# Spreading query and key halves over partitions by DMA, with the attention steps laid out anew

## The reference

```python
x = x + 0.5 * ffn(layernorm(x))      # silu(x W1^T) * (x W3^T), Walsh-Hadamard over 2048, times W2^T
x = x + attention(layernorm(x))
x = x + 0.5 * ffn(layernorm(x))

# attention, per head h and chunk; the weights are quantised to -1, 0, 1 times a scale
scores = einsum('bhtd,bhsd,hts->bhts', qi, ki, mask)      # mask: exp(-s_h (t - s)) below the diagonal
intra  = einsum('bhts,bhsd->bhtd', scores, vi)
cross  = einsum('bhtd,ht,bhde->bhte', qi, lam_t, S)
S      = lam_T * S + einsum('bhtd,ht,bhte->bhde', ki, lam_rev, vi)
out    = rmsnorm(rmsnorm(scale * (intra + cross))) @ proj^T
```

## Time and profile before

| | |
|---|---|
| profiled execution | 2532.32 us |
| its span, first to last instruction | 2530.6 us |
| median of three runs | 2535.62 us |
| TensorE matmul busy | 2385.3 us, 94% |
| VectorE busy | 1351.3 us, 53% |
| ScalarE busy | 873.9 us, 35% |
| mean granted TensorE clock | 0.987 |

### The profile page before, as it was taken

How to read it: one execution, slowest core, us unless ns; L and a number is a source line. 1 busy time by engine, 2 the same in 40 slices (tenths; PEclk the granted TensorE clock), 3 DMA queues, 4 the chain that set the end, 5 groups by cost and what they waited for, 6 DMA issues and landing times.

```text
span 2530.6 us, 32351 instructions
## 1 busy us (share of the span) xinstructions
PE 2385.3 (94%) x13040; PEld 1144.2 (45%) x13040; DVE 1351.3 (53%) x2599; ACT 873.9 (35%) x1461; POOL 161.5 (6%) x111
## 2 busy tenths in 40 slices
PE   5786999999999999999999999999999999989999
PEld 2243454445444454444544445444544445445444
DVE  6766565346644466335653466444664347557612
ACT  5545442234322352224522243223432245235211
POOL 4710000000000000000000000000000000000000
PEclk9898999999999999999999999999999999999999
DMA  7732002010012001100020100210002000100100
GB/s 218 178 109 57 1 1 50 17 34 1 17 34 34 17 1 32 36 17 17 1 51 17 34 1 5 46 26 25 1 17 49 19 17 1 34 17 1 34 17 17
DMA packets 184533, 82.58 MB, mean 33 GB/s; under 512 B 166080, under 2 KB 166080, under 8 KB 184384
## 3 DMA queue, kind: packets, MB, share of 16 engines
q1 hardware_dynamic: 184384, 80.51, 13.5%
HBM read 31.20 MB, written 8.39 MB: 16 GB/s over the span
## 4 chain that ended last, share of the span: by engine, by line
PE 77%; DVE 14%; issue 4%; DMA 2%; ACT 1%; POOL 1%; SPq 0%; POOLq 0%; DVEq 0%; ACTq 0%
PE l_bank L1262 23%; PE g_bank L1262 22%; PE d_bank L1277 22%; PE a_bank L1318 3%; DVE work L834 3%; PE a_bank L1304 2%; PE a_bank L1385 2%; DVE work L969 1%; PE a_bank L1372 1%; PE a_bank L1336 1%; DMA work<-cent 1%; DVE cent L1094 1%; PE a_bank L1366 1%; DVE stat L1031 1%; DVE stat L1028 1%
## 5 line engine op out<-in xcount | busy, mean ns | idle before, releaser
L1277 PE MATMUL d_bank<-w2t,work 128*128 128x512 f16 x2976 | 685.7, 381 | 10.9 <-DVE work L976 10.9
L969 DVE SCALAR_TENSOR_TENSOR work<-l_bank,l_scale,work 128x512 f32<-128x512 f32 x256 | 191.6, 749 | 649.0 <-PE l_bank L1262 647.6
L1277 PEld LDWEIGHTS d_bank<-w2t,work 128*128 128x128 f16 x2976 | 289.9, 98 | 352.7 <-DVE work L976 11.9
L1262 PE MATMUL l_bank<-xt,w3t 128*128 128x512 f16 x1728 | 404.5, 384 | 31.4 <-DVE work L969 31.4
L1262 PE MATMUL g_bank<-xt,w1t 128*128 128x512 f16 x1728 | 400.6, 382 | 19.6 <-ACT work L719 13.4
L719 ACT ACTIVATE work<-g_bank,g_scale 128x512 f32<-128x512 f32 x256 | 175.3, 685 | 506.9 <-PE g_bank L1262 504.1
L732 ACT CAST work<-work 128x512 f16<-128x512 f32 x248 | 153.2, 618 | 470.8 <-DVE work L969 469.6
L1262 PE MATMUL g_bank<-work,w1t 128*128 128x512 f16 x1344 | 308.4, 379 | 0.0
L1262 PE MATMUL l_bank<-work,w3t 128*128 128x512 f16 x1344 | 308.4, 379 | 0.0
L1262 PEld LDWEIGHTS l_bank<-xt,w3t 128*128 128x128 f16 x1728 | 168.1, 99 | 231.5 <-issue 45.1
L1262 PEld LDWEIGHTS g_bank<-xt,w1t 128*128 128x128 f16 x1728 | 167.4, 98 | 215.9 <-ACT work L719 13.0
(11 more groups left out here) (196 smaller groups left out, 1721.3 us busy)
## 6 DMA issues: line engine op xcount, KB each, us to landing
w2t<-in_L_ffn_W_dram SPq DMA_DIRECT2D x32, 256.0 KB, 3.3
xin<-in_L_attn_x_dram SPq DMA_DIRECT2D x8, 1024.0 KB, 5.2
out_dram<-work SPq DMA_DIRECT2D x7, 1024.0 KB, 4.3
work<-in_L_ffn_W_dram SPq DMA_DIRECT2D x8, 512.0 KB, 4.6
w2t<-in_L_attn_qkv_w_dram SPq DMA_DIRECT2D x6, 512.0 KB, 4.7
work<-in_L_attn_qkv_w_dram SPq DMA_DIRECT2D x3, 1024.0 KB, 7.9
mask<-in_L_attn_x_dram SPq DMA_DIRECT2D x1, 1024.0 KB, 5.7
w2t<-in_L_attn_proj_w_dram SPq DMA_DIRECT2D x2, 512.0 KB, 3.9
```

Of the source, the lines that this page charges most:

```text
L969: nc.vector.scalar_tensor_tensor(out=hfull, in0=l_bank[:], scalar=l_scale[:, j:j + 1], in1=gate, op0=ALU.mult, op1=ALU.mult).then_inc(hful ...
L1262: ins = nc.tensor.matmul(dst[:], wt[:, wp, k, P * j:P * (j + 1)], src[:, xp, k, :], start=(k == 0 and wp == xp), stop=(k == KT - 1 and wp ...
L1277: ins = nc.tensor.matmul(d_bank[t][:], parts[:, hp, P * t:P * (t + 1)], w2t[:, wp, j, :], start=(j == 0 and hp == wp), stop=(j == HT - 1 a ...
```

## The change

q_parts, k_parts and kT become buffers of their own. The two halves of q and of k are each stored to a DRAM buffer by SyncE (256 KB), and loaded from there three times each into 32 partitions of qs or ks (128 KB). The loads of a group wait until the last score of the group before has been computed. For groups 1 to 3, q moves to the slot of the group before's score 1, k to the slot of its score 2, and the low half of k to that of score 3. In group 0 the four value steps come before kturn and the first score. The attention starts its first score one slot later. The list NORM goes; its steps stand in the first three slots of the first attention block, as in the last one.

```diff
@@ -94,8 +94,10 @@
         sc = at["sc"].bitcast(F16).rearrange("p (b a h t) -> p b a h t", b=2, a=2, h=HG)
-        q_parts = sc[:, 0].rearrange("p a h t -> p a (h t)")
-        k_parts = sc[:, 1].rearrange("p a h t -> p a (h t)")
+        q_parts = sb("q_parts", [P, 2, T], F16)
+        k_parts = sb("k_parts", [P, 2, T], F16)
+        kT = sb("kT", [P, T])
+        parts_dram = nc.dram_tensor("parts_dram", [2, 2, P, 2, T], F16, kind="Internal").ap()
         def values(buffer):
...
@@ -233,18 +236,18 @@
         def attention_slots(at):
             slots = {}
-            start = at + 4
+            start = at + 5
             for g in range(GROUPS):
                 b = start + (3 + TT) * g
-                lead = b - 4 if g == 0 else b - 3
-                add(slots, lead, [("q", g)])
-                add(slots, lead + 1, [("qlow", g), ("k", g)])
-                add(slots, lead + 2, [("klow", g), ("kturn", g)])
+                lead = 6 if g else 5
+                add(slots, b - lead, [("q", g)])
+                add(slots, b - lead + 1, [("qlow", g), ("k", g)])
+                add(slots, b - lead + 2, [("klow", g)])
                 if g == 0:
-                    add(slots, b - 1, [("v", 0), ("v", 1)])
+                    add(slots, b - 3, [("v", 0), ("v", 1)])
+                    add(slots, b - 2, [("v", 2), ("v", 3)])
+                add(slots, b - 1, [("kturn", g)])
                 add(slots, b, [("score", (g, 0))])
-                if g == 0:
-                    add(slots, b, [("v", 2), ("v", 3)])
                 add(slots, b + 1, [("kv", g), ("score", (g, 1)), ("state", g)])
                 for c in range(TT):
                     add(slots, b + 2 + c, [("pv", (g, c))] + ([("score", (g, c + 2))] if c < TT - 2 else []))
@@ -274,7 +277,7 @@
                 add(slots, at + 5, tr1)
             return slots
-        def last_attention_slots():
+        def late_attention_slots():
             slots = attention_slots(4)
             pre, tr0, tr1 = norm_steps("qkv")
             return {**slots, 0: pre, 1: tr0, 2: tr1}
@@ -338,12 +341,11 @@
             return steps + [("resid", ("ffn1", t)) for t in range(TT)]
         FIRST = first_steps()
-        WITH_FIRST_ATTENTION = feed_forward("ffn1", attention_slots(4))
+        WITH_FIRST_ATTENTION = feed_forward("ffn1", late_attention_slots())
         WITH_ATTENTION = feed_forward("ffn1", attention_slots(0))
         SECOND = feed_forward("ffn2", second_slots())
-        SECOND_WITH_ATTENTION = feed_forward("ffn2", last_attention_slots())
+        SECOND_WITH_ATTENTION = feed_forward("ffn2", late_attention_slots())
         LAST = feed_forward("ffn2", {})
-        NORM = [step for steps in norm_steps("qkv") for step in steps]
         def bank_use(step, arg):
@@ -414,7 +416,7 @@
             return isinstance(v, int) and v <= 0
-        PLAN = [(FIRST, dict()), (NORM, dict(ffn=1))]
+        PLAN = [(FIRST, dict())]
         for i in range(1, B):
             PLAN.append((WITH_FIRST_ATTENTION if i == 1 else WITH_ATTENTION, dict(ffn=2 * i - 1, attn=i - 1, block=i, loaded=i)))
@@ -524,6 +526,33 @@
                         sp.wait_ge(res_done, TT * (place.ffn + 1))
                         sp.dma_start(out_tiles[bass.ds(place.block * TT, TT)].rearrange("t p d -> p t d"), x2).then_inc(y_stored, 16)
+                    elif step == "qlow":
+                        ag = place.attn * GROUPS + arg
+                        sp.wait_ge(q_lo, ag + 1)
+                        if ag >= 2:
+
+                            sp.wait_ge(q_moved, 16 * BLOCKS * (ag - 1))
+                        sp.dma_start(parts_dram[ag % 2, 0], q_parts[:]).then_inc(q_stored, 16)
+                    elif step == "klow":
+                        g = arg
+                        ag = place.attn * GROUPS + g
+                        sp.wait_ge(k_lo, ag + 1)
+                        if ag >= 2:
+
+                            sp.wait_ge(k_moved, 16 * BLOCKS * (ag - 1))
+                        sp.dma_start(parts_dram[ag % 2, 1], k_parts[:]).then_inc(k_stored, 16)
+                        if g:
+
+                            b, fill = place.filled("score", (g - 1, TT - 1))
+                            sp.wait_ge(a_ready[b], fill)
+                        sp.wait_ge(q_stored, 16 * (ag + 1))
+                        for i, part in enumerate((0, 1, 0)):
+                            sp.dma_start(qs[HD * i:HD * (i + 1)],
+                                         parts_dram[ag % 2, 0, :, part].rearrange("(h p) t -> p h t", h=HG)).then_inc(q_moved, 16)
+                        sp.wait_ge(k_stored, 16 * (ag + 1))
+                        for i, part in enumerate((0, 0, 1)):
+                            sp.dma_start(ks[HD * i:HD * (i + 1)],
+                                         parts_dram[ag % 2, 1, :, part].rearrange("(h p) t -> p h t", h=HG)).then_inc(k_moved, 16)
                     elif step == "split":
                         which, t = arg
                         m = place.norm[which]
...
@@ -763,22 +786,22 @@
                         nc.scalar.mul(qT[:], a_bank[b][:], QKV_SCALE / X_SCALE).then_inc(a_free[b], 1)
                         act.wait_ge(a_free[b], place.copied(step, arg, b) + 1)
+                        if ag:
+                            act.wait_ge(q_stored, 16 * ag)
                         nc.scalar.copy(q_parts[:, 0, :], qT[:]).then_inc(q_hi, 1)
-                        act.wait_ge(q_hi, ag + 1)
-                        move_high(q_parts, qs).then_inc(q_moved, 1)
                     elif step == "k":
                         b, fill = place.filled(step, arg)
                         ag = place.attn * GROUPS + arg
                         act.wait_ge(a_ready[b], fill)
                         if not known_zero(ag):
-                            act.wait_ge(sc_lo, TT * ag)
-                        nc.scalar.mul(flow, a_bank[b][:], QKV_SCALE / X_SCALE).then_inc(a_free[b], 1)
+                            act.wait_ge(kd_lo, ag)
+                        nc.scalar.mul(kT[:], a_bank[b][:], QKV_SCALE / X_SCALE).then_inc(a_free[b], 1)
                         act.wait_ge(a_free[b], place.copied(step, arg, b) + 1)
-                        nc.scalar.copy(k_parts[:, 0, :], flow).then_inc(k_hi, 1)
-                        act.wait_ge(k_hi, ag + 1)
-                        move_high(k_parts, ks).then_inc(k_moved, 1)
+                        if ag:
+                            act.wait_ge(k_stored, 16 * ag)
+                        nc.scalar.copy(k_parts[:, 0, :], kT[:]).then_inc(k_hi, 1)
                     elif step == "v":
                         t = arg
                         b, fill = place.filled(step, arg)
...
@@ -1057,10 +1074,10 @@
                         m = place.norm[which]
                         src = norm_source(place, which)[:, t, :]
                         dve.wait_ge(ln_rstd, m + 1)
-                        if place.steps is NORM:
+                        if place.steps is WITH_FIRST_ATTENTION and (which, t) == ("qkv", 0):
                             for b in range(2):
-                                dve.wait_ge(a_free[b], place.copied(step, arg, b))
+                                dve.wait_ge(a_free[b], place.copies[b])
                         if t and not (place.steps is FIRST and which == "ffn1"):
@@ -1109,17 +1126,11 @@
                         ag = a * GROUPS + arg
                         dve.wait_ge(q_hi, ag + 1)
                         nc.vector.tensor_tensor(q_parts[:, 1, :], qT[:], q_parts[:, 0, :], ALU.subtract).then_inc(q_lo, 1)
-                        move(q_parts, qs, 2, 0)
-                        dve.wait_ge(q_lo, ag + 1)
-                        move(q_parts, qs, 1, 1).then_inc(q_moved, 1)
                     elif step == "klow":
                         ag = a * GROUPS + arg
                         dve.wait_ge(k_hi, ag + 1)
-                        nc.vector.tensor_tensor(k_parts[:, 1, :], flow, k_parts[:, 0, :], ALU.subtract).then_inc(k_lo, 1)
-                        move(k_parts, ks, 1, 0)
-                        dve.wait_ge(k_lo, ag + 1)
-                        move(k_parts, ks, 2, 1).then_inc(k_moved, 1)
+                        nc.vector.tensor_tensor(k_parts[:, 1, :], kT[:], k_parts[:, 0, :], ALU.subtract).then_inc(k_lo, 1)
                     elif step == "v":
                         t = arg
...
                         n_sc = TT * (a * GROUPS + g) + c
                         b, fill = place.filled(step, arg)
                         dve.wait_ge(a_ready[b], fill)
-                        if c:
+                        if n_sc:
                             dve.wait_ge(sc_lo, n_sc)
-                        else:
-                            dve.wait_ge(kd_lo, a * GROUPS + (g + 1))
                         masked = flow.rearrange("p (h t) -> p h t", h=HG)
                         nc.vector.scalar_tensor_tensor(out=masked, in0=a_bank[b][:].rearrange("p (h t) -> p h t", h=HG),
```

(14 more changed lines are left out.)

9 lines of the change are left out of this document (5 added, 4 removed).

## The result

The changed kernel takes 2547.60 us (median of five, 2546.31 to 2551.20) against 2535.62: a ratio of 1.005, 95% interval 1.0036 to 1.0065. That is 12.0 us slower, where +2.4 was forecast; it lies in the stated range of 2527 to 2557, but beyond the likeliest case's own 2531 to 2545.

What follows compares the result with a forecast made beforehand. The prediction took TensorE's in-order queue as the bound, so only its waits count: 53.8 - 46.6 - 3.2 - 1.6 = +2.4 us, 2534.7 on the profiled execution, about 2538 against the median 2535.62; range 2527 to 2557.

Steps and rivals of the forecast that it cites:

- the likeliest case: Whole kernel: the forecast sum holds, +2.4 us, about 2538 us, own range 2531 to 2545; chance 0.58.
- the clock: Rival, whole kernel: more short TensorE stops in each attention drop the clock once in each, +19 us, 2557; chance 0.05.
- The 48 bank waits, +53.8: Groups 1 to 3, all eight attentions: q and k directly behind a score in a_bank0 wait for VectorE, 53.8 us lost.
- The waits removed, -46.6: TensorE's waits on partition copies, values and middle-block projections go: 42 waits, 39.5 us shown plus 7.1 beside, 46.6 us saved.
- The transfers, 0: Score 0 of groups 1 to 3: store and loads land before TensorE needs them, hidden by 2.4 us, so no cost.
- The first attention, -3.2: First attention block: with block 0's norm woven in, gate 0 to the down step behind q becomes like the last, 3.2 us saved.
- The tails, -1.6: Ends of the first and last attention blocks: the second norm moves one slot towards the end, 0.8 us saved each, 1.6 together.
- No transfer was late: Rival at score 0 of groups 1 to 3: loads 1.4 us late, 24 times, +34 us, 2572; chance 0.14.
- the norm of block 0 did not disappear: Rival, first attention: that norm vanishes under the first two main pairs, saving 14.0 rather than 3.2 us, 2527; chance 0.14.
- the bank waits came: Rival at q and k: the bank waits do not come because something lies between, -53.8 us, 2484; chance 0.03.

Runs made afterwards that it cites:

- Run 2: Changed kernel with q of groups 1 to 3 ahead of kv and score 1, k ahead of pv 0 and score 2, not behind the score: 2517.10 us, 0.993 of before.
- run 5: Changed kernel with all four projections in one slot and the second feed-forward's norm one slot earlier: 2558.64 us, 1.009 of before.
- run 8: Changed kernel with q of groups 1 to 3 ahead of pv 1 and score 3, k and its low half behind pv 2: 2504.07 us, 0.9879 of before.
- Run 6: Kernel before the change with only the norm of block 0 woven into the first attention block, NORM gone: 2531.44 us, 0.9985 of before.
- run 3: Changed kernel with q and k of groups 1 to 3 back in the slots of the kernel before, still moved by DMA: 2588.70 us, 1.021 of before.
- run 7: run 5 with q of groups 1 to 3 ahead of pv 1 and score 3, k and its low half behind pv 2: 2519.93 us, 0.9936 of before.
- the earlier form of run 10: Kernel before, engine copies kept, with early values, attention one slot later, block 0's norm woven in, four projections in one slot: 2525.12 us, 0.9957 of before.
- run 10: run 4 and Run 6 together, engine copies kept, value 1 ahead of value 0, second norm one slot earlier in middle blocks: 2512.08 us, 0.991 of before.
- run 4: Kernel before, engine copies kept, with attention one slot later and group 0's values before the first score: 2516.56 us, 0.9924 of before.

## Why the prediction was right and where it was wrong

**The number.** 2547.60 is in the range, but the outcome held likeliest, the same time within 5 us (0.50), did not come; that of slower by over 5 us had 0.27. The range reaches to 2557 because of a rival, the clock, that did not happen, so that it holds the measured time is in part luck. The four terms of the sum were close in size; what failed is something put at nothing, the norm behind the later attention in the middle blocks.

**The 48 bank waits, +53.8.** Right. The list shows 45.8 in 48, where some 45 was forecast; by place 1.02 for q after gate and down and 1.18 after lin, 0.79 and 0.92 for k, each 0.16 to 0.18 below the 1.19, 1.36, 0.95 and 1.08 of the prediction, which count the late end of a matmul too. k waits, for instance, like this:

```profile
941.87 0.38 PE L1345 MATMUL a_bank<-work 96*128 96x128 f16 x4
943.04 1.90 PE L1327 MATMUL a_bank<-zt,wqkv 128*128 128x512 f16 x8 [0.79 <-DVE work L1170]
```

943.04 less 941.87 less 0.22 is 0.95. Run 2 confirms the sum from the other side. The Trainium skill's rule on PSUM banks (Perfetto Trace Analysis, Matmuls) that was weighed there agrees with runs 5 and 8: a projection put behind another in the same bank waited 2.1 us, and with q and k no longer directly behind a score the 45.8 us of bank waits became 4.3, of a score behind q. Run 2 adds what the rule does not say: with the bank unchanged, the order alone was worth 30.5 us.

**The waits removed, -46.6.** The waits named did go, all but 1.8 of the 39.5 us shown. What failed is the step "In these six blocks the attention ends one slot later in the pattern gate, lin, down. That is the place of the pattern that the first attention block has now, where the projection starts with no wait". It followed the slot's place as far as the projection, where it was right, and stopped there. The norm behind the projection moved a main step nearer to the end of the feed-forward as well, and had no room: 1.54 us in each middle block, 9.2 in all. I had counted this norm in the late blocks, where a wait at the end was in a row, and took it as free in the middle ones, where none was. No row of waits showed it because its slack was just enough: silu done at 1010.37, gate at 1011.32.

**The transfers, 0.** Right, and with about the room that was said. SyncE in the changed kernel, and the score that needs the loads:

```profile
896.18 0.34 SPq L543 DMA_DIRECT2D parts_dram<-k_parts  x1
896.61 1.37 SPq L550 DMA_DIRECT2D work<-parts_dram  x3
898.44 1.89 SPq L554 DMA_DIRECT2D work<-parts_dram  x3
...
905.01 0.39 PE L1345 MATMUL a_bank<-work 96*128 96x128 f16 x4
```

The last load is issued by 900.3 and lands 2.6 later (the median of 192), some 2 us before the score.

**The first attention, -3.2.** The step was right:

```profile
236.17 2.75 PE L1271 MATMUL g_bank<-xt,w1t 128*128 128x512 f16 x12
...
259.15 3.48 PE L1286 MATMUL d_bank<-w2t,work 128*128 128x512 f16 x12
```

22.98 us against 23.04 forecast and 26.22 before; the down step then takes 0.73 more (3.48 in place of 2.75). Run 6 measures 4.0 (1.5 to 6.1 by its interval).

**The tails, -1.6.** The waits fell from 5.4 and 5.6 to 4.5 and 4.6, -1.9. The step behind them ran 0.2 quicker in the first attention and 0.7 slower in the last, so that -1.3 is left in these two traces.

**The rivals.** No transfer was late, the norm of block 0 did not disappear (9.1 us for zt stand twice), the bank waits came. On the clock: the granted clock stayed at 1.00 over the stretch of each attention that holds the stops of 0.8 to 1.2 us, so the rule by which this rival would have been the likely one is not borne out here; runs 3, 5 and 7 show slow steps behind longer stops.

**Open.** Why the clock fell behind five of six waits of 2.1 us in run 7, behind two of six of the same wait in run 5, and behind one of twelve of 2.1 to 2.7 us in run 3, is not known.

## What to carry to other kernels

When a step moves, follow everything that hangs behind it to the end of its stage, and read the slack there, not only the waits: a chain that is just in time has no row in the list of waits. The order within a slot matters as much as the slot: with a matmul group put ahead of a short one in the same bank TensorE waited 0.2 to 0.4 us, behind it 0.8 to 1.2. Work taken from engines that are not the bound was worth only the waits that it ended, here 19 us, and the layout decided whether they ended or moved.

## What the hardware showed that I had not expected

- A short stop has two prices. Forty-eight stops of 0.8 to 1.2 us left the granted clock at 1.00. Behind stops of 2.07 to 2.16 us the projection took 5.31 in place of 3.63 us, in five blocks of six in run 7 and in two of six both in run 5 and in the earlier form of run 10; behind twelve stops of a score of 2.1 to 2.7 us only one step ran slowly, and behind all six of 4.1 to 4.3 (run 3, middle blocks).
- The way through DRAM is short: 2.0 to 2.1 us for a store of 256 KB and 2.6 for a load of 128 KB into 32 partitions, though the loads are made of packets of about 1 KB: the change adds 24,576 packets of 512 B to 2 KB, 128 for each of the 192 loads. SyncE issues three such loads in 1.25 to 1.40 us in 58 of 64 cases, and in up to 2.35 in the others.
- The start of the first attention's first gate varies by 3.8 us over the thirteen traces (233.79 to 237.60), and by 3.3 between two whose code is the same up to there (233.79 before, 237.09 in run 4): more than the forecast's whole sum. Two traces of different kernels are best compared block by block.
